# A one-core attention and gated MLP layer: transfers of the first pair reordered, its square layers split into two flagged stages each, two blocks' queries split earlier

## What is computed

```
x = layernorm(x + attn(x))      # linear attention: Q (K^T V) sqrt(3/D) Wo^T, x is 4096 x 256, D = 64
x = layernorm(x + ffn(x))
ffn: h = silu(x W1^T * s1) * (x W2^T * s2)    # 256 -> 1024
     h = gelu(h H1^T * h1_s)                  # 1024 -> 1024, the first square layer
     h = gelu(h H2^T * h2_s)                  # 1024 -> 1024, the second square layer
     return h W3^T * s3                       # 1024 -> 256
```

## Time and profile before

| | |
|---|---|
| median of 3 runs | 658.0 us (657.55 to 658.16) |
| the profiled execution's own time | 660.88 us |
| its span in the trace | 659.0 us, 9226 instructions |
| PE busy | 639.4 us, 97% of the span |
| DVE, ACT, POOL busy | 477.1, 411.3, 279.3 us |
| moved by the DMA engines | 103.89 MB |

### The profile page before, as it was taken

The page is one execution under the profiler, slowest core; times in us unless marked ns, Lnnn a source line. Parts: engine busy times, 40 slices in busy tenths (PEclk is TensorE's granted clock), DMA queues, the critical chain, the costliest instruction groups (busy, mean ns, idle before and its releaser), DMA issues.

```text
span 659.0 us, 9226 instructions
## 1 busy us (share of the span) xinstructions
PE 639.4 (97%) x3187; PEld 536.0 (81%) x3187; DVE 477.1 (72%) x713; ACT 411.3 (62%) x696; POOL 279.3 (42%) x226
## 2 busy tenths in 40 slices
PE   9989888999999999999999999999999999999995
PEld 7868676887879888888889888888888888888885
DVE  4576565798755898598755899598746799488476
ACT  5479786857863557656763457655764456666654
POOL 0367799188000466069000367059000268069024
PEclk9999998999999999999999999999999999999999
DMA  8989899953330025734330015734340005534201
GB/s 318 379 337 354 308 377 355 345 193 128 128 130 1 1 70 160 258 128 176 133 132 1 1 35 170 274 128 142 132 174 1 0 8 185 191 128 146 111 1 66
DMA packets 24370, 103.89 MB, mean 158 GB/s; under 512 B 2224, under 2 KB 3312, under 8 KB 16496
## 3 DMA queue, kind: packets, MB, share of 16 engines
q1 hardware_dynamic: 24032, 102.98, 44.1%
q10 hardware_dynamic: 288, 0.26, 0.1%
HBM read 87.51 MB, written 23.07 MB: 168 GB/s over the span
## 4 chain that ended last, share of the span: by engine, by line
PE 72%; DVE 3%; POOL 1%; issue 1%; ACT 1%; POOLq 0%; DVEq 0%; ACTq 0%
PE ps L1285 48%; PE ps L1233 13%; PE ps L1331 8%; DVE R L925 1%; DVE xr L909 1%; PE ps L1165 1%; PE ps L1153 1%; PE ps L1354 0%; ACT R L663 0%; DVE U L944 0%; POOL rstd L476 0%; POOL quarter L504 0%; ACT quarter L709 0%; POOL rstd L447 0%; POOL quarter L513 0%
## 5 line engine op out<-in xcount | busy, mean ns | idle before, releaser
L1285 PE MATMUL ps<-R,ring 128*128 128x512 f32 x1792 | 411.2, 391 | 5.3 <-issue 4.2
L1285 PEld LDWEIGHTS ps<-R,ring 128*128 128x128 f32 x1792 | 336.5, 188 | 75.7 <-issue 4.6
L925 DVE TENSOR_TENSOR R<-quarter,R 128x512 fp32r<-128x512 f32 x284 | 250.4, 903 | 69.7 <-ACT R L663 69.5
L663 ACT CAST R<-quarter 128x512 fp32r<-128x512 f32 x288 | 175.3, 615 | 31.0 <-POOL quarter L504 12.0
L1233 PE MATMUL ps<-x1T,w 128*128 128x512 f32 x512 | 119.6, 392 | 1.2 <-issue 0.6
L709 ACT ACTIVATE quarter<-U,sc 128x512 f32<-128x512 f32 x96 | 69.5, 723 | 72.9 <-DVE U L944 32.1
L1233 PEld LDWEIGHTS ps<-x1T,w 128*128 128x128 f32 x512 | 95.2, 188 | 23.4 <-ACT sg L629 1.7
L494 POOL TENSOR_TENSOR quarter<-quarter,quarter 128x512 f32<-128x512 f32 x32 | 49.2, 1538 | 103.0 <-ACT quarter L709 96.4
L629 ACT ACTIVATE sg<-ps,sc 128x512 f32<-128x512 f32 x64 | 43.9, 689 | 62.8 <-PE ps L1233 62.7
L445 POOL TENSOR_TENSOR ve<-mv,eps 128x4 f32<-128x4 f32 x14 | 5.7, 405 | 181.9 <-DVE mv L902 181.9
L679 ACT COPY U<-ps 128x512 f32<-128x512 f32 x96 | 56.3, 586 | 36.8 <-PE ps L1285 35.0
(11 more groups left out here) (84 smaller groups left out, 373.1 us busy)
## 6 DMA issues: line engine op xcount, KB each, us to landing
ring<-combos SPq DMA_DIRECT2D x56, 1024.0 KB, 4.9
combos<-unit SPq DMA_DIRECT2D x8, 1024.0 KB, 9.0
unit<-in_h1T SPq DMA_DIRECT2D x4, 1024.0 KB, 14.0
xr<-in_x_rows SPq DMA_DIRECT2D x8, 512.0 KB, 5.0
unit<-in_h2T SPq DMA_DIRECT2D x4, 1024.0 KB, 8.4
xT<-in_xT SPq DMA_DIRECT2D x7, 512.0 KB, 8.0
out<-xr SPq DMA_DIRECT2D x7, 512.0 KB, 2.9
w<-w_dram SPq DMA_DIRECT2D x3, 1024.0 KB, 7.6
```

Of the source, the lines that this page charges most:

```text
L663: nc.scalar.copy(R[slot_of(p, u)][:, 0, c, :], quarter[operand_home(p, u)][:, c, :]).then_inc(hi_done, 1)
L925: nc.vector.tensor_tensor(r[:, 1, c, :], quarter[operand_home(p, u)][:, c, :], r[:, 0, c, :].bitcast(f32), ALU.subtract).then_inc(lo_done, 1)
L1285: last = nc.tensor.matmul(ps[:, bank + j, :], w, view(R[slot_of(p, u)][:, part, k, :]), start=n in (0, 1, 5) and k == 0 and part == 0, sto ...
```

## The change

It has six parts.

1. SP's order for pair 0 is written out anew (rows below). The relay of H1's corners stands ahead of unit 4, unit 5 behind rings 0 and 1, units 6 and 7 around ring 2, and the relay of H2's corners and that of W3 behind ring 3 and ring 9.
2. Each square layer of pair 0 becomes two stages, `without_sums` (products 0 and 1) and `with_sums` (2 to 6), and there are seven flags. `lowf` keeps the columns of whole units apart from those of sums.
3. Blocks 2 and 3's queries are split within `first_l1`, in block 0's loop. `beside4` and `beside5` move to the free halves of two `xr` tiles, and `load_rows_late` loads the rows of blocks 2 and 3 once these are stored.
4. POOL makes unit 4's sums right after unit 3's, ahead of the first differences, not between the two groups of differences.
5. ACT's readings of low halves move: unit 4 whole into block 1's loop, sums of unit 3 behind it, sums of unit 4 into the copies of layer 0, sums of unit 7 to just ahead of the last `gelu` group.
6. In the front DVE splits x of the last block (`low_x(7)`) before it waits for the product of energy and Wo.

```
-FLAGS = 5
+FLAGS = 7
...
-        beside_at = (c11_at, ..., c11_at + 6144, qs_at, qs_at + 2048, sg_at + 2048, sg_at)
+        rows_at = [xr_at + 4096 * b + 2048 for b in (2, 3)]
+        beside_at = (c11_at, ..., c11_at + 6144, *rows_at, sg_at + 2048, sg_at)
...
+            def load_rows_late(b):
+                sp.wait_ge(qlo_done, b + 1)
+                sp.wait_ge(unit_out[b + 2], UNIT_STORED)
+                sp.wait_ge(bits_done, n_bits("sums", b + 2))
+                load_rows(b)
...
+            relay_hidden(0)
             load_unit(4)
-            relay_hidden(0)
...
+            store_unit(4)
+            load_ring(3)
             relay_hidden(1)
+            load_ring(4)
+            load_rows_late(2)
+            load_ring(5)
+            store_unit(5)
...
             combine(2)
             combine(3)
+            combine(4)
             for p in range(NP):
                 differences(p, 0)
                 if p > 0:
                     inverse_deviation(1, 2 * p)
-                else:
-                    combine(KH)
...
# DVE, front
+            low_x(NB - 1)
             dve.wait_ge(t1_ready, 1)
-            low_x(NB - 1)
...
# PE
             def flag_sum(s):
-                pe.wait_ge(bits_done, (n_bits("wq", 0), n_bits("w12", 3), n_bits("sums", KH - 1), n_bits("sums", NU - 1), n_bits("w3", 1))[s])
+                pe.wait_ge(bits_done, n_bits(*(("wq", 0), ("w12", 3), ("whole", KH - 1), ("sums", KH - 1), ("whole", NU - 1),
+                                               ("sums", NU - 1), ("w3", 1))[s]))
...
                 for j in range(KH):
+                    if L == 0 and n == 0 and j == KH - 1:
+                        pe.wait_ge(h_made, 2 * HC)
+                        flag_sum(3)
                     if L == 0 and n == 6 and j == KH - 1:
                         pe.wait_ge(sum_done[0], 3)
-                        flag_sum(3)
+                        flag_sum(4)
+                    if L == 1 and n == 1 and j == 0:
+                        pe.wait_ge(add_done, n_add(0, 2, KH - 1))
+                        flag_sum(5)
+                    if L < 2 and n == 1 and j == KH - 1:
+                        pe.wait_ge(fsum_done, 4 + 2 * L)
...
-            stages_from(0, (front, first_l1, lambda view: hidden(0, 0, view), lambda view: hidden(0, 1, view)))
+            stages_from(0, (front, first_l1, lambda view: without_sums(0, 0, view), lambda view: with_sums(0, 0, view),
+                            lambda view: without_sums(0, 1, view), lambda view: with_sums(0, 1, view)))
```

More of the change, by code:

```diff
@@ L35 @@
 BIT_ORDER = [("wq", 0), ("whole", 0), *[("w12", i) for i in range(4)], ("whole", 1), ("whole", 2), ("sums", 0), ("whole", 3),
-             ("sums", 1), ("sums", 2), ("sums", 3), ("whole", 4), ("whole", 5), ("sums", 4),
+             ("sums", 1), ("whole", 4), ("sums", 2), ("sums", 3), ("whole", 5), ("sums", 4),
              ("whole", 6), ("whole", 7), ("sums", 5), ("sums", 6), ("sums", 7), ("w3", 0), ("w3", 1)]
@@ L112, in build @@
         R = [sb(f"R{i}", [P, 2, KH, BLK], f32r) for i in range(SLOTS)]
+        xr_at = top[0]
         xr = sb("xr", [P, 4, TPB * E])
@@ L361, in _ @@
             load_ring(1)
+            load_unit(5)
             store_unit(3)
+            load_unit(6)
             load_ring(2)
-            load_unit(6)
             load_unit(7)
+            store_unit(4)
+            load_ring(3)
             relay_hidden(1)
-            sp.dma_start(w3_dram, w3_src).then_inc(w3_relayed, 16)
-            for p in range(NP):
+            load_ring(4)
+            load_rows_late(2)
+            load_ring(5)
+            store_unit(5)
+            load_ring(6)
+            store_unit(6)
+            load_ring(7)
+            load_rows_late(3)
+            store_unit(7)
+            load_ring(8)
+            load_ring(9)
+            sp.dma_start(w3_dram, w3_src).then_inc(w3_relayed, 16)
+            load_ring(10)
+            sp.wait_ge(w3_relayed, 16)
+            sp.wait_ge(unit_out[5], UNIT_STORED)
+            sp.wait_ge(bits_done, n_bits("sums", 5))
+            sp.dma_start(w3[:, :, :].rearrange("p k e -> p (k e)").bitcast(f32), w3_dram).then_inc(w3_in, 16)
+            for g in range(11, 17):
+                load_ring(g)
+            for p in range(1, NP):
                 g = 2 * NPROD * p
                 load_ring(g + 3)
[L372 to L375, removed]
+                store_block(2 * p - 2)
                 load_ring(g + 4)
[L377 to L381, removed]
+                store_block(2 * p - 1)
+                if p < NP - 1:
+                    sp.wait_ge(stored[0], 16 * p)
+                    load_q(2 * p + 2)
                 load_ring(g + 5)
-                if 0 < p < NP - 1:
+                if p < NP - 1:
                     sp.wait_ge(stored[1], 16 * p)
                     load_q(2 * p + 3)
-                if p == 0:
-                    store_unit(5)
                 load_ring(g + 6)
-                if p == 0:
-                    store_unit(6)
                 if p < NP - 1:
@@ L577, in bits_of_whole @@
                 act.wait_ge(unit_in[i], 16)
-                bits(unit[i][:, 0:3:2, :].bitcast(u16).rearrange("p a (n two) -> p a n two", two=2)[:, :, :, 0], 1 + i // KH, 3 * (i % KH))
+                bits(unit[i][:, 0:3:2, :].bitcast(u16).rearrange("p a (n two) -> p a n two", two=2)[:, :, :, 0], 1 + i // KH, i % KH)
             def bits_of_sums(i, parts=range(2)):
@@ L727, in hidden @@
                     hi(p, u0 + 4, j)
+                    if L == 0 and 1 <= j <= 2:
+                        bits_of_sums(4, range(j - 1, j))
                 if L == 0:
-                    bits_of_whole(7)
+                    bits_of_whole(6)
                 for j in range(KH):
@@ L732, in hidden @@
                     hi(p, u0 + 5, j)
+                    if L == 0 and j == 1:
+                        bits_of_whole(7)
                 if L == 0:
@@ L745, in hidden @@
                     bits_of_sums(6)
-                    bits_of_sums(7)
                 if L == 1:
@@ L799, in _ @@
                 silu(0, j, A)
+                if j == 1:
+                    hi_of_q(2)
+                if j == 3:
+                    hi_of_q(3)
                 if j == 0:
@@ L954, in hidden @@
                     lo(p, u0 + 2, j)
+                    if L == 0 and j == 1:
+                        flag_out(3)
+                    if L == 1 and j == KH - 1:
+                        flag_out(5)
                 for j in range(KH + 1):
@@ L1290, in hidden, with without_sums, with_sums @@
             def hidden(p, l, view):
+                without_sums(p, l, view)
+                with_sums(p, l, view)
+            def without_sums(p, l, view):
+                product(p, l, 0, view)
+                product(p, l, 1, view)
+            def with_sums(p, l, view):
                 L = 2 * p + l
@@ L1293, in hidden @@
                 a, b = 2 * p + 2, 2 * p + 3
-                for n in range(4):
-                    product(p, l, n, view)
+                product(p, l, 2, view)
+                product(p, l, 3, view)
                 if more and l == 1:
```

59 lines of the change are left out of this document (27 added, 32 removed).

## The result

The changed kernel takes 652.74 us (median of 4 runs, 652.57 to 653.65) where the kernel before took 658.08 beside it. The ratio is 0.9913, with a 95% interval of 0.9894 to 0.9932: 5.3 us faster, where 7.9 were forecast. Two later rounds of the same comparison gave 0.9924 (0.9901 to 0.9946) and 0.9906 (0.9887 to 0.9924). The profiled execution took 653.65 us with a span of 651.9.

What follows compares the result with a forecast made beforehand. PE, busy for 97% of the span, was taken to bound the kernel; 0.3 + 2.1 + 6.0 - 0.3 - 0.1 - 0.1 = 7.9 us took the median from 658.0 to 650.1 us, range 647.5 to 654.

Steps and rivals of the forecast that it cites:

- forecast A: Both stalls go and nothing takes their place: 7 to 9.5 us less, 648.5 to 651 us; chance 0.55.
- rival B: The wait moves to ring 4 behind the relay or silus behind unit 4's load: 651 to 656 us; chance 0.29.
- the silu behind unit 4: Block 1's loop: ACT's reading waits 0 to 1 us for unit 4's load, and PE waits for the silus behind.
- So the stall is worth 6.0 us.: PE's wait for ring 3 ahead of product 3: 4.2 us plus 1.8 of low clock, all to go.
- The 2.1 us go: PE's wait at flag 2 in the first layer's last tiles goes: gain 2.1 us, product 0 starts near 73.
- Ring 3's margin of 4 us: Ring 3, issued at 80.3, lands near 91 us; product 3 is due at 95.
- ring 4's of 1: Ring 4 behind H2's relay lands at 101 us, product 4 due at 102.3; 0.3 us charged, 3 as bound.
- Two more stages: Added stages and flags, with loads, branches and small sums: 0.1 us charged for both, 1.2 as bound.
- Sums of unit 7: ACT's reading ahead of the last gelus takes 2.75 us against 2.66 idle there: costs 0.1 us, without slack.
- T1s: DVE's subtraction no longer stands between the product and T1s; PE's wait of 0.4 us bounds it: gain 0.3.
- Queries: Early split in block 0's loop, where DVE and ACT have idle time: 0 us, 3.5 on DVE without that cover.

Runs made afterwards that it cites:

- the transfers alone: Kernel before with the relays of H2's corners and of W3 issued behind ring 3: 656.50 us, ratio 0.9976 to the kernel before.
- the flag needing sums: Changed kernel with flag 2 waiting for H1's sums again and ACT reading unit 3's sums in block 1's loop: 657.34 us, 0.9981 to the kernel before.
- the run with the relays ahead: Changed kernel with the relays of H2's corners and W3 put back ahead of ring 3: 660.16 us, ratio 1.0026 to the kernel before.
- the run with flag 5 early: Changed kernel with DVE's operations for flag 5 ahead of the low parts of product 9's operand: 652.51 us, 0.9905 to the kernel before.

## Why the prediction was right, and where it was off

The direction, both removed waits and the range were right. The size was forecast at 7.9 us and is 5.3 (4.4 and 6.1 in the later rounds). The 652.7 us lie outside the 648.5 to 651 of the forecast A, "both stalls go and nothing takes their place", and within the 651 to 656 of rival B, which had a chance of 0.29. What rival B names happened in part (the silu behind unit 4), but most of the difference comes from the sizes of the terms. The sum took 6.0 us, read from an execution 2.9 us above the median, off the median. Beside it the prediction notes the 2.9 us, and doesn't ask whether the stall is in them.

- **"So the stall is worth 6.0 us."** The mechanism was right, the size was that of one execution. Between the two first traces the stretch from product 0 to the attention output fell by 5.6 us (49.60 to 43.99). Between the second traces of both it is 1.1 (45.07 to 43.97), and the transfers alone gave 1.6. This is the term that was mis-sized.
- **"The 2.1 us go", gain 2.1 at product 0.** The wait went, and the sum had no clock for it. Behind this wait three of four traces (second one of before, the transfers alone, the flag needing sums) have a clock of 0.50 to 0.62 and lose 1.6 to 2.5 us. What that is worth depends on the ring. With the relays ahead of ring 3 it is nothing, as product 3 starts when ring 3 lands, and the run with the relays ahead shows it. With ring 3 early, the flag waiting for the sums costs 3.7 us. So 6.0 and 2.1 were not two savings that add up, and the sum took them so. A new wait of 1.1 us came for the silu behind unit 4's reading, forecast at 0 to 1. From the start of the first layer to product 0 it took 33.7 and 35.2 us in the two traces of the kernel before and 32.8 to 33.2 in three of the changed kernel: 0.9 less between the first traces, 2.1 less between the later ones, where the low clock is in the difference.
- **Ring 3's margin of 4 us, ring 4's of 1.** 1.8 and 0.8. Ring 3 was issued at 81.77 and not at 80.3, and took 12.2 us and not 10.8. Rival B's stall at ring 4 didn't come. Its other half, the silu behind unit 4, did. Ring 4 took 13.3 us behind the relay, where ring 2 took 5.3 with a part of unit 6 ahead of it. The second part of the relay was issued at 82.8 and took 17.1 us, to 99.9, and ring 4 landed behind it, at 102.3. With this agrees the rule that a completion count lands only after every earlier write of the same DMA engine (the Trainium skill, "DMA: Bandwidth & Descriptors", "Queues, rings and completion order").
- **Two more stages, "0.1 for both".** The boundaries cost nothing to be seen. But "flags' inputs are ready" overlooked that a flag's sum holds the PSUM bank of product 8's last chunk until DVE has read it, and DVE reads it behind product 9's low parts: 1.16 us. It cost nothing to be seen, since the 1.03 us ahead of product 10 went for it, as the run with flag 5 early shows. The forecast had that wait staying.
- **Sums of unit 7, 0.1.** The first of the last gelus starts at 126.54, 6.9 us before the 133.44 of the earlier trace rows, as does all of PE there: 0.
- **T1s, 0.3.** The wait is gone. What it gained was not measured by itself.
- **Queries, 0.** The early split costs nothing to be seen in the first layer. That it allows the rows to be loaded earlier was overlooked: together the two are worth 3.3 us against a late split with the rows behind ring 7.

## What to carry to other kernels

Take a second trace before a term is sized by a wait and what follows it. Here one execution had 1.8 us of low clock behind the ring and none behind the flag, the next the reverse. Two waits in a row on one engine are not two savings: in one round the relays moved alone gave 1.6 us, the rest of the change without them lost 2.1, and the whole gave 4.4. The same holds for a low clock: it counts only where no later wait takes it in. Where a small result borrows a PSUM bank, look up who frees it and what stands ahead of that on its engine, not only who reads it, even if it cost nothing to be seen here.

## What the hardware showed that was not expected

The same wait of 2.1 us on PE was followed by a clock of 1.00 in one execution and of 0.54 and 0.61 in the next. In the three traces with longer waits (3.3, 4.2 and 4.9 us) a low clock followed, and one execution of the kernel before, with 1.3 us of wait ahead of product 3, had none there. That it follows each time isn't shown. The changed kernel with the flag waiting for the sums has a wait of 3.3 us in its trace and a mean clock of 0.992, but two of its twelve runs have 0.998, as the kernels without such a wait. What decides it stays open.
